# Delta-rule stage of a fused decoder: products of the next half ahead of the formings, two coupling buffers

## The chip, the cores and the metric

The kernel runs on one core of a Trainium2 chip. The metric is device time in microseconds for one launch, which is one program of fifteen stages over 16 batch rows of 128 tokens by 256 channels, all in float32 unless said. Only the first stage, `delta_stage` (L0_attn), is changed. In the profile PE is TensorE, PEld its weight load, DVE VectorE, ACT ScalarE and POOL GpSimd.

## What is computed

The first stage is a gated delta rule with 8 heads, 8 decay modes and key and value width 64:

```python
qr = _l2norm(_rotary(q, cos, sin)) * scale
kr = _l2norm(_rotary(k, cos, sin))
g = jnp.log(jnp.clip(tg * rho, 1e-06))
...
def step(S, inp):
    q_t, k_t, v_t, b_g, b_beta = inp
    S = S * jnp.exp(b_g)[..., None, None]
    kv = jnp.einsum('mbhk,mbhkv->mbhv', k_t, S)
    dv = (v_t[None] - kv) * b_beta[..., None]
    S = S + k_t[..., :, None] * dv[..., None, :]
    o_t = jnp.einsum('mbhk,mbhkv->mbhv', q_t, S)
    return (S, o_t)
...
o = jnp.einsum('tmbhv,hm->bthv', ys, mode_w)
return (o * gate).reshape(B, T, H * DV) @ Wo
```

The kernel does not scan over time. For each head and mode (a "chain") it forms a 128x128 matrix of decayed key-key products N and one of decayed key-query products, solves the unit triangular system with N in four blocks of 32 rows, and multiplies the solution by the query products.

## The kernel before

A turn of the stage is one batch row. A turn has two halves of 4 heads, so 32 chains each, in 8 groups of 4 chains (`GROUPS`). Halves are numbered `u`, and half `u` of a turn is first (`hf` 0) or second (`hf` 1). Every engine has its own program, and semaphores order them. A half passes through these steps:

- **Products** (`phase`): DVE rotates keys and queries (`rotate`, L1153 and L1158), POOL adds the two parts (`add_halves`, L698), PE makes decay exponents (L823, L824, L827) that ACT exponentiates (`decays`, L1019), PE makes the products (L844), and DVE multiplies both into the buffer `NB` (`take_products`, L1172). A pack is two groups. DVE issues `rotate(p+1, 0)`, group 2p, `rotate(p+1, 1)`, group 2p+1.
- **Lower blocks** (`take_lower`, ACT L1029): copies the 32x32 diagonal blocks, half after group 3 and half after group 7.
- **Inversion** (`invert`, DVE L1201 to L1210): a transpose, a copy, 60 linked small operations (L1207 and L1208 in turn) and a transpose back. In a first half, steps for the next batch row stand between the links.
- **Spread** (ACT L1039): puts the inverses into `Df`.
- **Forming** (`form`, PE L811, into PSUM banks 6 and 7): inverse times both matrices, one group at a time. ACT takes each group (`take_formed`, L1007 and three L1011): outputs to `NB`, couplings to the tensor `couplings`. One group must be taken before the next is formed.
- **Couplings, solutions** (`couple`, PE L736 and L863; ACT L1046): three block rows times four heads.
- **Outputs** (`output`, PE L878), `gated` (DVE L1218) and, once a turn, `project_out` (PE L886).

There is one N buffer, `NB[:, 0]`, so group i of half u+1 may be written only after group i of half u is formed (the wait on `formed` in `take_products`). PE therefore alternates: `form(u, i)`, `phase(u+1, i)`. The projections of the next batch row (`project_qk` L750, `project_bt` L756, `turn_qk` L775, `sum_logs` L765 to L767, `swap` L782, `project_v` L789, `project_gates` L797) stand among the couplings and outputs. POOL fills the right-hand sides (`fill`, L690) when the outputs of the half before are done. The order in each engine's program is written out by hand in its `turn`.

## Time and profile before

| | us |
|---|---|
| median of 3 runs | 6814.46 (6813.0 to 6816.96) |
| the profiled execution | 6818.27 |
| its span | 6816.5 |
| first stage, to its last `project_out` | about 2405 of the span |
| PE, DVE, ACT, POOL busy | 77%, 52%, 31%, 16% of the span |

The profiled execution is 3.8 us above the median. The first stage is about 35% of the span. Its steady part repeats once a batch row, and the page's shares mix it with fourteen other stages, so it is read from the timeline.

### The profile page before, as it was taken

What the parts mean: (1) busy time and instruction counts of PE and PEld (TensorE: products, weight loads), DVE (VectorE), ACT (ScalarE), POOL (GpSimd) and SP (SyncE); (2) the same over time, 40 slices, a digit from 0 to 9 for tenths busy, and PEclk for the clock granted to TensorE, in tenths of its full rate; (3) what the DMA queues carried; (4) which work ended last, traced back from release to release, by engine and by line L of the source; (5) the groups of instructions that cost most, each with busy time, mean ns of one, the idle gap of its engine ahead of it and who ended that gap; (6) DMA issues with size and microseconds to landing.
All of it is one profiled execution on the core that took longest, in us unless ns stands there. A gap on an engine that the chain in (4) does not pass through costs nothing. (4 is left out here: it accounts for less than half of the span.)

```text
span 6816.5 us, 79744 instructions
## 1 busy us (share of the span) xinstructions
PE 5226.9 (77%) x28029; PEld 3625.2 (53%) x28132; DVE 3569.8 (52%) x7608; ACT 2091.8 (31%) x3626; POOL 1070.7 (16%) x846
## 2 busy tenths in 40 slices
PE   2878878788787775999997877467577467788698
PEld 1666656666565544666665555234355245555454
DVE  6777777777777532000015545558734535444444
ACT  2544545454454411212212222211023322232111
POOL 1222222222222121000002222000011012221000
PEclk8988989889898886999998878655578578789799
DMA  0000000000000000000000000000000000000000
GB/s 32 1 1 1 1 2 1 1 1 2 1 1 1 1 23 36 13 25 12 25 0 7 0 29 6 11 3 1 10 25 1 4 8 0 21 6 1 12 18 24
DMA packets 13528, 63.44 MB, mean 9 GB/s; under 512 B 1168, under 2 KB 5648, under 8 KB 11152
## 3 DMA queue, kind: packets, MB, share of 16 engines
q1 hardware_dynamic: 13200, 59.17, 2.5%
q8 instruction: 193, 3.16, 0.2%
q14 instruction: 135, 1.11, 0.1%
HBM read 57.07 MB, written 2.10 MB: 9 GB/s over the span
## 5 line engine op out<-in xcount | busy, mean ns | idle before, releaser
L1467 PE MATMUL psum<-arena 128*128 128x512 f32 x1600 | 707.0, 596 | 58.4 <-DVE Y L1531 35.8
L811 PE MATMUL psum<-arena 128*128 128x256 f32 x2048 | 546.4, 413 | 140.7 <-ACT arena L1039 131.7
L1548 DVE SCALAR_TENSOR_TENSOR Y<-psum,arena,Y 128x256 f32<-128x256 f32 x416 | 172.5, 477 | 847.8 <-PE psum L1479 847.8
L1479 PE MATMUL psum<-arena 128*128 128x256 f32 x2624 | 583.0, 380 | 4.1 <-DVE arena L1572 4.1
L1479 PEld LDWEIGHTS psum<-arena 128*128 128x128 f32 x2624 | 499.1, 190 | 111.7 <-issue 43.5
L811 PEld LDWEIGHTS psum<-arena 128*128 128x128 f32 x2048 | 392.3, 202 | 288.9 <-issue 167.2
L144 POOL TENSOR_TENSOR arena<-arena,eps 128x4 f32<-128x4 f32 (+2 forms) x76 | 15.0, 197 | 3341.4 <-DVE arena L139 3341.4
L1467 PEld LDWEIGHTS psum<-arena 128*128 128x128 f32 x1600 | 304.5, 191 | 409.4 <-issue 341.7
L1172 DVE TENSOR_TENSOR arena<-psum,arena 128x1024 f32<-128x1024 f32 x256 | 313.3, 1224 | 392.0 <-PE psum L844 204.6
L698 POOL TENSOR_TENSOR arena<-arena 128x512 f32<-128x512 f32 x256 | 341.8, 1356 | 713.2 <-DVE arena L1158 713.2
L863 PE MATMUL psum<-arena 64*32 64x64 f32 (+2 forms) x6144 | 414.6, 220 | 0.0
L1513 ACT ACTIVATE arena<-psum,arena 128x512 f32<-128x512 f32 x256 | 175.9, 687 | 701.4 <-PE psum L1467 701.4
L422 PE MATMUL psum<-ident,arena 128*128 128x128 f32 x1280 | 216.9, 324 | 211.5 <-ACT arena L493 211.5
L402 PE MATMUL psum<-arena 128*128 128x512 f32 x640 | 358.9, 694 | 16.8 <-ACT arena L482 11.2
L863 PEld LDWEIGHTS psum<-arena 64*32 64x32 f32 (+2 forms) x6144 | 352.6, 109 | 20.7 <-issue 12.7
L1208 DVE TENSOR_TENSOR weights<-weights 128x30 f32<-128x30 f32 (+14 forms) x960 | 343.8, 358 | 32.6 <-DVE weights L1207 2.5
L1207 DVE TENSOR_TENSOR weights<-weights 128x30 f32<-128x30 f32 (+14 forms) x960 | 341.4, 356 | 34.9
L414 PEld LDWEIGHTS psum<-arena 128*128 128x128 f32 x2048 | 283.6, 216 | 102.3 <-issue 62.5
L844 PE MATMUL psum<-arena 64*128 64x256 f32 x2048 | 294.2, 406 | 28.1 <-POOL arena L698 28.1
L300 POOL TENSOR_TENSOR arena<-arena,weights 128x1024 f32<-128x1024 f32 x128 | 242.2, 1900 | 408.3 <-PE psum L402 343.1
L422 PEld LDWEIGHTS psum<-ident,arena 128*128 128x128 f32 x1280 | 178.1, 171 | 233.8 <-ACT arena L493 233.5
L414 PE MATMUL psum<-arena 128*128 128x17 f32 x2048 | 275.2, 278 | 33.4 <-ACT arena L490 33.4
(436 smaller groups left out, 8839.0 us busy)
## 6 DMA issues: line engine op xcount, KB each, us to landing
arena<-in_experts_L_ffn SPq DMA_DIRECT2D x8, 2052.0 KB, 8.5
arena<-in_ctxT SPq DMA_DIRECT2D x16, 512.0 KB, 3.3
arena<-in_experts_L_ffn SPq DMA_DIRECT2D x18, 384.0 KB, 3.1
weights<-in_w_L_attn SPq DMA_DIRECT2D x1, 3106.0 KB, 13.2
weights<-in_w_L_ffn SPq DMA_DIRECT2D x1, 3072.0 KB, 10.0
weights<-in_w_L_ffn SPq DMA_DIRECT2D x1, 2753.0 KB, 13.3
weights<-in_w_L_relu SPq DMA_DIRECT2D x1, 2436.0 KB, 8.9
X<-in_x SPq DMA_DIRECT2D x1, 2048.0 KB, 8.2
```

What stands on the lines that cost most here:

```text
L402: mm = nc.tensor.matmul(out[:, b * 4:b * 4 + 4, :], qT[:, c, u * P:(u + 1) * P], km[:, at % 2, b * 4:b * 4 + 4, :], start=True, stop=True)
L414: mm = nc.tensor.matmul(o_psum[:, c * HH + h, :], pT[:, j % 2, h, :], v, start=True, stop=True)
L422: mm = nc.tensor.transpose(pt_psum[:, h, :], pr[:, j % 2, h, :], k.ident[:, :])
L698: pool.tensor_tensor(both_, both_, t1[:, j, :, :], ALU.add).then_inc(s["rotated"], 1)
L811: mm = nc.tensor.matmul(ps[:, 6 + j // 2, (j % 2) * 2 * P:(j % 2 + 1) * 2 * P], Df[:, c, :], both(hf)[:, :, c, :], start=True, stop=True)
L844: mm = nc.tensor.matmul(ps[:, bank, m * 2 * P:(m + 1) * 2 * P], kq[rows, i // 2 % 2, at, 0, :], kq[rows, i // 2 % 2, at, :, :], start=True ...
L863: mm = nc.tensor.matmul(ps[n:n + Q, 4 + h, m * DK:(m + 1) * DK], couplings[0:n + Q, place(h, m), n - Q:n], ur[0:n + Q, h, m, :], start=Tru ...
L1172: dve.tensor_tensor(both(hf)[:, :, group, :].rearrange("p k c t -> p c k t"), products, bc(NB[:, 1 + hf, group, :], 2, 2), ALU.mult).then_ ...
L1207: linked(dve.tensor_tensor(part, bc(lanes[:, j + 1:, j], 2, j), bc(inv[:, j, 0:j], 1, below), ALU.mult))
L1208: linked(dve.tensor_tensor(inv[:, j + 1:, 0:j], inv[:, j + 1:, 0:j], part, ALU.add))
L1467: mm = nc.tensor.matmul(ps[:, bank, :], W[s][name][:, c, f * P:(f + 1) * P], xT[:, g, c, :], start=(c == 0), stop=(c == C - 1))
L1479: mm = nc.tensor.matmul(out, h[:, m % 2, f, u * P:(u + 1) * P], W[s]["w2"][:, f, :], start=(f == 0), stop=(f == FC - 1))
```

## The change

- `NB` has four planes in place of three, an N and an output plane for each half of a turn. `couplings` is gone: `take_formed` writes the couplings over N in the same plane, and a new `set_identities` (ACT, three copies of 32x1024) writes the identity blocks once a half. The wait of `take_products` on `formed` is gone.
- PE runs all 8 groups of `phase(u+1)` with only two formings of half u in them (behind groups 2 and 5). The other six formings follow the phase, with projections between them, and the couplings come behind these. ACT's order follows.
- `invert` works in place on `inv`, without the copy L1202. Its in-between steps stand at other links, and `first_part` and `second_part` move into it.
- POOL runs `add_halves` before `fill` in both halves.
- `xs` and `xT` move to the rest of the weights' region, and the stage's first memset and the three copies of L956 go.

In the diff `...` marks what is left out (renamed buffers in the same instructions).

```diff
-    xs, xT = A(D), A(C, P)
+    used = (k.words(stage) + 7) // 8 * 8
+    own = Arena(k.regions[k.stages.index(stage) % 2][:, used:], REGION - used)
+    xs, xT = own(D), own(C, P)
     v, gateT, bt, logs = A(W), A(PAIRS, P), A(2 * DHEADS * M), A(2 * DHEADS * M)
     qkT, qkS = A(2, PAIRS, P), A(2, PAIRS, P)
     kq, t1 = A(2, 4, 2, P), A(2, 4, P)
-    NB = A(1 + HALVES, CH, P)
-    couplings, Df = A(CH, P - Q), A(CH, P)
+    NB = A(2 * HALVES, CH, P)
+    Df = A(CH, P)
...
-        return NB[:, 0:hf + 2:hf + 1, :, :]
+        return NB[:, 2 * hf:2 * hf + 2, :, :]
...
+                add_halves(u + 1)
                 fill(u, g, 0)
-                add_halves(u + 1)
...
-                fill(u + 1, g, 1)
                 if more:
                     add_halves(u + 2)
+                fill(u + 1, g, 1)
...
-                    pe.wait_ge(s["outputs_formed"], u * GROUPS + i)
                     pe.wait_ge(s["couplings_formed"], u * GROUPS + i)
...
-                        pe.wait_ge(s["outputs_formed"], (u + 1) * GROUPS)
                         pe.wait_ge(s["couplings_formed"], (u + 1) * GROUPS)
+                        pe.wait_ge(s["identities_set"], u + 1)
...
-                                              couplings[0:n + Q, place(h, m), n - Q:n], ur[0:n + Q, h, m, :],
+                                              NB[0:n + Q, 2 * (u_odd), place(h, m), n:n + Q], ur[0:n + Q, h, m, :],
...
                 for i in range(GROUPS):
-                    form(u, 0, i)
                     phase(g, u + 1, 1, i)
+                    if i in (2, 5):
+                        form(u, 0, i // 3)
                 if more:
                     turn_x(g + 1)
-                couple(u, 1, (u + 1) * GROUPS + GROUPS - 1)
+                form(u, 0, 2)
+                form(u, 0, 3)
                 if more:
                     project_qk(g + 1)
-                couple(u, 2)
+                form(u, 0, 4)
                 if more:
                     project_bt(g + 1)
-                couple(u, 3)
+                for i in range(5, GROUPS):
+                    form(u, 0, i)
+                couple(u, 0, 1, (u + 1) * GROUPS + GROUPS - 1)
                 if more:
                     turn_qk(g + 1)
-                output(u, g, 0, 0)
+                couple(u, 0, 2)
                 if more:
                     sum_logs(g + 1)
+                    swap(g + 1)
+                couple(u, 0, 3)
+                output(u, g, 0, 0)
                 output(u, g, 0, 1)
-                if more:
-                    swap(g + 1)
                 for i in range(GROUPS):
-                    form(u + 1, 1, i)
                     if more:
                         phase(g + 1, u + 2, 0, i)
-                couple(u + 1, 1, (u + 2) * GROUPS + GROUPS - 1 if more else None)
-                if more:
-                    project_v(g + 1)
-                couple(u + 1, 2)
-                if more:
-                    project_gates(g + 1, (u + 3) * GROUPS)
-                couple(u + 1, 3)
+                    if i in (2, 5):
+                        form(u + 1, 1, i // 3)
+                for i in range(2, GROUPS):
+                    form(u + 1, 1, i)
+                    if more and i == 4:
+                        project_v(g + 1)
+                    if more and i == 6:
+                        project_gates(g + 1, (u + 3) * GROUPS)
+                couple(u + 1, 1, 1, (u + 2) * GROUPS + GROUPS - 1 if more else None)
+                couple(u + 1, 1, 2)
+                couple(u + 1, 1, 3)
                 output(u + 1, g, 1, 0)
                 output(u + 1, g, 1, 1)
...
-            for q in range(1, NQ):
-                rows = slice(q * Q, (q + 1) * Q)
-                nc.scalar.copy(couplings[rows, :, (q - 1) * Q:q * Q], bc(k.ident[rows, rows], 1, CH))
...
-                nc.scalar.copy(NB[:, 1 + hf, 4 * i:4 * i + 4, :], formed[:, :, 1, :]).then_inc(s["outputs_formed"], 1)
-                if i == 0:
-                    need(act, "solution_ready", u * (NQ - 1) * HALF)
+                nc.scalar.copy(NB[:, 2 * hf + 1, 4 * i:4 * i + 4, :], formed[:, :, 1, :])
...
-                    a = nc.scalar.copy(couplings[0:q * Q, 4 * i:4 * i + 4, (q - 1) * Q:q * Q],
+                    a = nc.scalar.copy(NB[0:q * Q, 2 * hf, 4 * i:4 * i + 4, q * Q:(q + 1) * Q],
                                        formed[0:q * Q, :, 0, q * Q:(q + 1) * Q])
...
-                if x == 0:
-                    need(act, "inverse_turned", n)
...
-                    a = nc.scalar.activation(lower[rows, 16 * x:16 * (x + 1), :], N_[rows, 16 * x:16 * (x + 1), rows],
+                    a = nc.scalar.activation(diagonal[rows, 16 * x:16 * (x + 1), :], NB[rows, 2 * hf, 16 * x:16 * (x + 1), rows],
...
+            def set_identities(n, hf):
+
+                act.wait_ge(s["lower_taken"], (n + 1) * 2)
+                for q in range(1, NQ):
+                    rows = slice(q * Q, (q + 1) * Q)
+                    a = nc.scalar.copy(NB[rows, 2 * hf, :, rows], bc(k.ident[rows, rows], 1, CH))
+                a.then_inc(s["identities_set"], 1)
...
-                    a = nc.scalar.copy(Df[rows, :, rows], Dc[rows, :, :])
+                    a = nc.scalar.copy(Df[rows, :, rows], diagonal[rows, :, :])
...
                 for i in range(GROUPS):
-                    take_formed(u, 0, i)
                     decays(u + 1, 1, i)
+                    if i in (2, 5):
+                        take_formed(u, 0, i // 3)
                     if i == 5:
-                        take_lower(u + 1, 0)
+                        take_lower(u + 1, 1, 0)
                 if more:
                     take_x(g + 1)
-                take_lower(u + 1, 1)
+                take_lower(u + 1, 1, 1)
+                take_formed(u, 0, 2)
+                take_formed(u, 0, 3)
+                if more:
+                    square(g + 1)
+                take_formed(u, 0, 4)
+                if more:
+                    sigmoids(g + 1)
+                for i in range(5, GROUPS):
+                    take_formed(u, 0, i)
+                if more:
+                    logarithms(g + 1)
+                set_identities(u + 1, 1)
                 solutions(u, 1)
                 if more:
-                    square(g + 1)
+                    take(g + 1, qkT, "qk_turned", "qkT_ready")
                 solutions(u, 2)
                 if more:
-                    sigmoids(g + 1)
-                solutions(u, 3)
-                if more:
-                    logarithms(g + 1)
-                    take(g + 1, qkT, "qk_turned", "qkT_ready")
                     round_sums(g + 1)
                     round_rest(g + 1)
                     take(g + 1, qkS, "swapped", "swapped_ready")
+                solutions(u, 3)
                 spread(u + 1)
                 for i in range(GROUPS):
-                    take_formed(u + 1, 1, i)
                     if more:
                         decays(u + 2, 0, i)
-                        if i == 5:
-                            take_lower(u + 2, 0)
+                    if i in (2, 5):
+                        take_formed(u + 1, 1, i // 3)
+                    if more and i == 5:
+                        take_lower(u + 2, 0, 0)
                 if more:
-                    take_lower(u + 2, 1)
+                    take_lower(u + 2, 0, 1)
+                for i in range(2, GROUPS):
+                    take_formed(u + 1, 1, i)
+                    if more and i == 4:
+                        take_v(g + 1)
+                if more:
+                    set_identities(u + 2, 0)
                 solutions(u + 1, 1)
-                if more:
-                    take_v(g + 1)
                 solutions(u + 1, 2)
                 solutions(u + 1, 3)
                 if more:
...
-                if not isinstance(n, int) or n:
-                    dve.wait_ge(s["formed"], (n - 1) * GROUPS + i + 1)
-                    if i == 0:
-                        need(dve, "lower_taken", n * 2)
...
-                need(dve, "inverse_ready", n)
-                linked(dve.transpose(lanes[:, :, :], lower.rearrange("p c t -> p t c")))
-                linked(dve.tensor_copy(inv[:, :, :], lanes[:, :, :]))
+                linked(dve.transpose(inv[:, :, :], diagonal.rearrange("p c t -> p t c")))
...
-                    linked(dve.tensor_tensor(part, bc(lanes[:, j + 1:, j], 2, j), bc(inv[:, j, 0:j], 1, below), ALU.mult))
+                    linked(dve.tensor_tensor(part, bc(inv[:, j + 1:, j], 2, j), bc(inv[:, j, 0:j], 1, below), ALU.mult))
...
-                dve.transpose(Dc.rearrange("p c j -> p j c"), inv[:, :, :].rearrange("p i j -> p j i")
+                dve.transpose(diagonal.rearrange("p c j -> p j c"), inv[:, :, :].rearrange("p i j -> p j i")
                               ).then_inc(s["inverse_turned"], 1)
 
             def gated(g, hf):
@@ -1301,18 +1316,16 @@
                     state["ch"].end()
                 steps = []
                 if more:
-                    steps += [(12, lambda: sum_squares(g + 1)), (34, lambda: scale_decays(g + 1)),
-                              (36, lambda: clip_decays(g + 1)), (40, lambda: normalise(g + 1)),
-                              (52, remember("views", lambda: split(g + 1))),
-                              (54, lambda: split_rest(g + 1, state["views"]))]
+                    steps += [(18, lambda: sum_squares(g + 1)), (20, lambda: scale_decays(g + 1)),
+                              (22, lambda: clip_decays(g + 1)), (32, lambda: normalise(g + 1)),
+                              (36, remember("views", lambda: split(g + 1))),
+                              (38, lambda: split_rest(g + 1, state["views"])),
+                              (50, lambda: first_part(g + 1)), (58, lambda: second_part(g + 1))]
                 if not first:
-                    steps += [(2, remember("ch", lambda: finish(g - 1))), (20, applied)]
+                    steps += [(2, remember("ch", lambda: finish(g - 1))), (14, applied)]
                 invert(u + 1, between(*sorted(steps, key=lambda x: x[0])))
-                if more:
-                    first_part(g + 1)
                 gated(g, 0)
                 if more:
-                    second_part(g + 1)
                     phase(g + 1, u + 2, 0)
                     invert(u + 2)
                 gated(g, 1)
```

PE, end of the first half's products, before: a forming and a group of products alternate, and the couplings (L736, L863) come directly behind `turn_x` (L742).

```order
L811 MATMUL psum<-arena 128x256 x4
L822 REGISTER_ALU
L823 MATMUL psum<-arena 128x512
L824 MATMUL psum<-arena,weights 128x512
L827 MATMUL psum<-weights,arena 128x128 x4
L844 MATMUL psum<-arena 128x256 x4
L739 REGISTER_ALU
L623 ISA
L742 MATMUL psum<-ident,arena 128x128 x2
L854 ISA
L736 MATMUL psum<-arena 128x1
L863 MATMUL psum<-arena 32x64 x8
```

The same place on PE in the changed kernel, where L841 is the products, L808 a forming, L748 `project_qk`:

```order
L841 MATMUL psum<-arena 128x256 x4
L737 REGISTER_ALU
L623 ISA
L740 MATMUL psum<-ident,weights 128x128 x2
L805 REGISTER_ALU
L808 MATMUL psum<-arena 128x256 x4
L805 REGISTER_ALU
L808 MATMUL psum<-arena 128x256 x4
L748 MATMUL psum<-weights 128x512 x4
L805 REGISTER_ALU
L808 MATMUL psum<-arena 128x256 x4
L754 MATMUL psum<-weights 128x128 x2
```

Three more formings stand behind these rows, and then the couplings.

PE, end of the second half's products in the changed kernel (L787 `project_v`, L795 `project_gates`, L734 and L860 a coupling; one row x12 is three formings):

```order
L841 MATMUL psum<-arena 128x256 x4
L808 MATMUL psum<-arena 128x256 x12
L784 REGISTER_ALU
L787 MATMUL psum<-weights 128x512 x2
L808 MATMUL psum<-arena 128x256 x8
L623 ISA
L795 MATMUL psum<-weights 128x128 x8
L808 MATMUL psum<-arena 128x256 x4
L734 MATMUL psum<-arena 128x1
L860 MATMUL psum<-arena 32x64 x8
```

Six formings now stand between the products and the couplings, where before one stood in front of each group.

ACT, end of a second half, before (L1029 `take_lower`, L1046 solutions, L1039 spread, L1000 gates):

```order
L1011 COPY arena<-psum 32x4x32
L1011 COPY arena<-psum 64x4x32
L1011 COPY arena<-psum 96x4x32
L1019 ACTIVATE arena<-psum 128x512
L1029 ACTIVATE weights<-arena 32x512 x4
L1046 ACTIVATE arena<-psum 32x512 x4
L995 COPY arena<-psum 128x512
L1046 ACTIVATE arena<-psum 32x512 x8
L1039 COPY arena<-weights 32x32x32 x4
```

ACT at the same place in the changed kernel (L1036 `set_identities`, L1052 solutions, L1045 spread):

```order
L1009 COPY arena<-psum 128x512
L1011 COPY arena<-psum 32x4x32
L1011 COPY arena<-psum 64x4x32
L1011 COPY arena<-psum 96x4x32
L1036 COPY arena<-ident 32x32x32 x3
L1052 ACTIVATE arena<-psum 32x512 x12
L1045 COPY arena<-weights 32x32x32 x4
L1002 ACT_TABLE_LOAD
L1002 ACTIVATE arena<-psum 128x512
```

The six takings stand between `take_lower` and the solutions, and the spread is behind them all.

## Rows read from the trace of the kernel before

**Rows 1.** DVE timeline: start us, length us, engine, line, operation, out<-in [idle before <-releaser]

```profile
1047.56 1.95 DVE L1201 STREAM_TRANSPOSE weights<-weights 128x1024 f32<-128x1024 f32 x1 [2.61 <-ACT weights L1029]
...
1091.93 1.23 DVE L1172 TENSOR_TENSOR arena<-psum,arena 128x1024 f32<-128x1024 f32 x1 [3.29 <-ACT arena L1019]
...
1116.54 1.22 DVE L1172 TENSOR_TENSOR arena<-psum,arena 128x1024 f32<-128x1024 f32 x1 [2.07 <-PE psum L844]
1120.38 1.97 DVE L1201 STREAM_TRANSPOSE weights<-weights 128x1024 f32<-128x1024 f32 x1 [2.61 <-ACT weights L1029]
...
1188.63 1.94 DVE L1201 STREAM_TRANSPOSE weights<-weights 128x1024 f32<-128x1024 f32 x1 [2.61 <-ACT weights L1029]
```

**Rows 2.** DVE timeline, end of a first, then a second half's inversion

```profile
1079.12 0.40 DVE L1218 SCALAR_TENSOR_TENSOR arena<-psum,arena 128x256 f32<-128x256 f32 x1
...
1122.38 0.69 DVE L1202 COPY weights<-weights 128x1024 f32<-128x1024 f32 x1
...
1137.33 0.40 DVE L1208 TENSOR_TENSOR weights<-weights 128x228 f32<-128x228 f32 x1
1137.76 1.11 DVE L1207 TENSOR_TENSOR weights<-weights 128x220 f32<-128x220 f32 x1
...
1149.98 0.38 DVE L1218 SCALAR_TENSOR_TENSOR arena<-psum,arena 128x256 f32<-128x256 f32 x1
1151.19 0.69 DVE L1153 TENSOR_TENSOR arena<-arena,weights 128x512 f32<-128x512 f32 x1 [0.83 <-issue]
```

**Rows 3.** PE timeline, the wait behind that inversion

```profile
1150.42 3.78 PE L886 MATMUL psum<-weights,arena 128*128 128x256 f32 x8 [13.16 <-DVE arena L1218]
```

**Rows 4.** timeline of all engines, the last half of the last turn

```profile
2366.60 1.97 PE L811 MATMUL psum<-arena 128*128 128x256 f32 x8 [1.23 <-ACT arena L1011]
2368.60 0.58 ACT L1007 COPY arena<-psum 128x512 f32<-128x512 f32 x1 [2.15 <-PE psum L811]
2369.08 0.57 ACT L1011 COPY arena<-psum 32x128 f32<-32x128 f32 x3
...
2369.80 1.97 PE L811 MATMUL psum<-arena 128*128 128x256 f32 x8 [1.24 <-ACT arena L1011]
...
2385.80 0.16 PE L736 MATMUL psum<-arena 128*128 128x1 bf16 x1 [1.24 <-ACT arena L1011]
...
2399.21 3.71 PE L878 MATMUL psum<-arena 128*64 128x128 f32 x64
...
2402.97 0.42 DVE L1218 SCALAR_TENSOR_TENSOR arena<-psum,arena 128x256 f32<-128x256 f32 x1 [50.39 <-PE psum L878]
```

**Rows 5.** timeline of all engines, one pack of products

```profile
1162.26 2.94 POOL L698 TENSOR_TENSOR arena<-arena 128x512 f32<-128x512 f32 x2 [5.62 <-DVE arena L1158]
...
1165.26 1.13 PE L844 MATMUL psum<-arena 64*128 64x256 f32 x8 [0.85 <-POOL arena L698]
...
1166.53 1.23 DVE L1172 TENSOR_TENSOR arena<-psum,arena 128x1024 f32<-128x1024 f32 x1 [0.78 <-PE psum L844]
...
1168.27 0.68 DVE L1158 TENSOR_TENSOR arena<-arena,Y 128x512 f32<-128x512 f32 x1
```

**Rows 6.** ACT timeline, the identity blocks at the stage's start

```profile
70.34 3.15 ACT L956 COPY arena<-ident 32x1024 f32<-32x1024 f32 x3
```

**Rows 7.** ACT timeline, the last `take_lower` before a second half's inversion

```profile
1117.80 2.55 ACT L1029 ACTIVATE weights<-arena 32x512 f32<-32x512 f32 x4 [1.44 <-DVE arena L1172]
```

**Rows 8.** groups of PE by line, 1047.5-1137.3 us (xcount | busy us, mean ns | idle)

```profile
L750 PE MATMUL psum<-weights,arena 128*128 128x512 f32 x8 | 3.7, 605 | 0.0
...
L797 PE MATMUL psum<-arena,weights 128*128 128x128 f32 x16 | 2.1, 281 | 0.0
L782 PE MATMUL psum<-arena,weights 128*128 128x512 f32 x4 | 2.0, 618 | 0.0
```

**Rows 9.** PE timeline, first forming behind a first half's inversion

```profile
1085.07 3.77 PE L811 MATMUL psum<-arena 128*128 128x256 f32 x8 [4.86 <-ACT arena L1039]
```

**Rows 10.** stretch: PE, PEld, DVE, ACT, POOL busy us (x), granted clock, DMA share, GB/s

```profile
1083.00:1085.50 2.50, 0.43 (x1) 0.43 (x2) 2.50 (x4) 1.92 (x2) 0.67 (x2) 0.50 0.00 0
```

27 lines of the change are left out of this document (12 added, 15 removed).

## The prediction

> **What bounds the kernel now.** I read the timeline of DVE first, since the stage repeats once a batch row. A second half's inversion starts 72.8 us behind a first half's, and the next first half's 68.25 us behind that [rows 1]. A turn is 141.1 us. Inside the second half, group 0 of the products is taken at 1091.93, group 7 at 1116.54, and the inversion starts 3.84 behind group 7: so 28.45 us from the first taking to the inversion [rows 1]. The inversion ends with L1218 at 1149.98, 29.6 us behind its start [rows 2], and PE waits 13.16 us for it [rows 3]. So one loop sets the time: products alternating with formings, `take_lower`, inversion, spread. The couplings and outputs of PE lie in the inversion's shade with 13 us to spare. The change takes the formings out of the products and puts six of eight into that shade. The question is whether the shade holds them.
>
> **What a forming costs alone.** The last half of the last turn shows it, since no products stand beside it there. Formings start 3.20 us apart, 1.97 on PE and the rest ACT's L1007 and L1011, because banks 6 and 7 must be emptied before the next [rows 4]. The first coupling starts 3.20 behind the last forming (2382.60, to 2385.80), the twelve head steps of couplings take 13.4 (2385.80 to 2399.21), and the outputs 3.76 to the start of L1218 [rows 4].
>
> **The new chain of PE and ACT in a second half**, counted from the inversion's start, which is the end of `take_lower` on ACT. ACT takes group 2, which PE formed while ACT was busy: 1.05, and PE starts group 3 at 1.2. Five formings at 3.20 are 16.0. `project_v` (the shape of L782, 2.0) and `project_gates` (2.1) [rows 8] stand between formings and mostly fill waits for ACT; past 1.2 us of wait each they cost 0.5, so 1.0. Couplings can start at 18.2. `set_identities` is three copies like L956, 3.15 us [rows 6], and holds the first solution back, but PE is busy 4.5 us with the first block row, so it costs nothing; with less cover it would cost 3.15. Couplings 13.4, outputs 3.76: o is ready at 35.4.
>
> The inversion itself becomes shorter: L1202 goes (0.77 from its start to the next link [rows 2]), and `fill` no longer runs under it. Under L690 four links take about 1.1 us where the link in front took 0.40 [rows 2], which is 2.9 us. It would end at 29.6 - 0.8 - 2.9 = 25.9. The chain ends 9.5 us later. DVE has `gated` in its queue in front of `rotate`, so the whole products phase of the next half stands behind the outputs. Those 3.7 us of DVE are worth nothing.
>
> The Trainium skill speaks of the same thing in "SBUF — State Buffer", section "SBUF: two separate sides": VectorE with two SBUF inputs and GpSimd take one port pair in turn, for the whole instruction. By the rows four links ran slower and none was held for good; either way a `fill` taken out of the inversion returns a few us there, all of it inside the 9.5 us of slack.
>
> From o ready: L1218 and the loop's end 1.2 (1149.98 to 1151.19 [rows 2]), two rotations of two instructions at 0.6, 2.4, and from the last rotation's end to the taking 4.35 (POOL starts 0.1 behind it at 1162.26 and takes 2.94, PE 1.13, the taking is at 1166.53 [rows 5]). Group 0 is taken at 35.4 + 8.0 = 43.4.
>
> **Products without formings.** They are not bound by PE now but by a loop through four engines. From the end of `rotate(p,1)` to the taking of the next pack's group it is 4.35, then the taking 1.14 and the next rotation 1.28: the next end is at 1168.95, so 6.75 a pack [rows 5], where before a pack took 2/7 of 24.6, 7.0 [rows 1]. Groups 0, 2 and 4 are taken at 0, 6.75 and 13.5. At group 5 ACT must wait for a forming, take it (1.05) and do a `take_lower` (2.55 [rows 7]) before the decay of group 6: forming ends 3.6 behind the taking of group 4, the copies at 4.7, `take_lower` at 7.2, decay at 7.8. Group 6 is taken at 7.9, group 7 (exponents 0.8, products 1.1) at 9.9. So group 7 at 23.4 and the inversion at 23.4 + 3.84 = 27.2, against 28.45. Freeing the products from the formings is worth 1.2 us a half.
>
> Second half: 43.4 + 27.2 = 70.6, before 68.25: **+2.3**.
>
> **First half.** Here `project_qk` (3.7) delays group 4 by 2.2 net; `project_bt` and the sigmoid are hidden by ACT's takings. Couplings can start at 1.2 + 16.0 + 2.2 = 19.4. Between them stand `turn_qk` (eight 128-column matmuls, half of L797's sixteen: 1.0), `sum_logs` (twelve: 1.5) and `swap` (L782, 1.85) [rows 8]. With 13.4 and 3.76 o is ready at 40.9. The inversion with its steps lasted 31.6 (1047.56 to L1218 at 1079.12 [rows 1, 2]); less 0.8 and with `first_part` and `second_part` inside it is some 32.6, and it must also wait for ACT's rounding of `sum_logs`, at about 31.5, which makes it 38. Still under 40.9. L1218 and start of the rotation 0.4, then 6.75: group 0 at 48.1, and with 27.2 it is 75.3, before 72.8: **+2.5**.
>
> **The clock.** All this is at the full 2.4 GHz. Before, PE ran without a gap in the products; the granted clock fell behind its waits for DVE: after 4.86 idle a forming took 3.77 instead of 1.97 [rows 4, 9], at a granted clock of 0.50 [rows 10]. The changed kernel has no 13 us wait, but in a first half PE waits about 5 us from its last output to the first product, in a second half about 3.5, in front of each pack about 3, and at `take_lower` 3. The first surely drops the clock, the others perhaps. A drop doubles L844 in the loop (1.1) or a forming in the chain (1.8). Bounds: nothing, where those costs lie in other waits, and 8 us a turn, if each of some six waits does it at 1.3. I take two drops a turn that cost: **+2.4**, nearer to the lower bound because in the last half formings kept the full clock across gaps of 1.24 us [rows 4].
>
> **The sum.** 2.3 + 2.5 + 2.4 = 7.2 us a turn, 15 times from the first inversion of turn 0 to the last: +108. At the ends: L956 goes from the start (3.15 [rows 6]), the first half has no chain in front of it (about -4), and the last half starts its formings at a better clock (two of them took double: -3.6). About -10. 6818.3 + 98 = 6916 in the profiled execution, 3.8 less in the median: **6912 us**.
>
> **The rivals.**
> 1. As forecast, the PE and ACT chain takes the place of the inversion as the bound, with some drops of the clock. 6912. Chance 0.50.
> 2. The same without further cost of the clock: 4.8 x 15 - 10 = +62: 6876. For it: no gap in the formings is above 2 us. Chance 0.20.
> 3. The clock falls in every pack. PE is busy 3.7 us and idle 3.05 in each, and a first half's wait of 4.86 was enough [rows 9]. Then 4.8 + 8 = 12.8 a turn, +182: 6996. The Trainium skill, "TensorE: Matmul & The Clock Gate", section "HAM oscillation", tells of a kernel that was throttled anew behind every wait between its bursts. Chance 0.15.
> 4. Faster: the chain fits under the inversion, and DVE stays the bound. Then the second half is 25.9 + 8.0 + 27.2 = 61.1 and the first 32.6 + 7.15 + 27.2 = 67.0, which is 13 a turn less: about 6610. It decides at a chain shorter by 9.5 us in the second half and 8.3 in the first; half of the way there, 2.4 us a half, is break-even. It needs formings at some 2 us apart, where [rows 4] have 3.20. A partial gain counts here. Chance 0.11.
> 5. No change: the longer chain and the shorter products cancel. Chance 0.04.
>
> **How the numbers follow.** The forecast is the likeliest case. The range takes cases 1 and 2 with 1 us a turn of doubt, and most of 3: 6860 to 6990. A measurement of this kernel can tell about 0.2% (14 us) from no change. Faster 0.11, same 0.04, slower 0.85.
>
> **What the changed profile would show.** L1201 starts about 75 and 71 us behind each other. L1218 waits for PE's L875, not at once behind the transpose, by some 9 us in a second half and 3 in a first. Formings L808 behind the products start 3.2 apart with gaps "<-ACT L1011". L1189 is spaced 6.8 a pack. L1223 and L1225 have no 1.1 us links. PE waits less than 6 us anywhere, and the granted clock says which of 1 to 3 it is. I am wrong if PE still waits for the inversion in a second half, if formings are closer than 3.2, or if DVE takes the products of a half in under 20 us.

## The result and the profile after

| | us |
|---|---|
| before, median of 3 | 6814.46 |
| after, median of 3 | 6987.04 (6981.84 to 7007.31) |
| ratio | 1.026, 95% interval 1.0228 to 1.0292 |
| profiled execution, its span | 7007.31, 7005.5 |
| forecast | 6912, range 6860 to 6990 |

The change makes the kernel slower, as forecast, but by 173 us where 98 were forecast. By the ratio to the kernel before the time is 1.026 x 6814 = 6991, which is just outside the range. The profiled execution was the slowest of the three.

I call the stretch that begins at an inversion with steps between its links a "first half" and the other one a "second half", as the prediction does. DVE's timeline of the changed kernel over one second half (columns as in [rows 1]):

```profile
1039.84 1.94 DVE L1217 STREAM_TRANSPOSE weights<-weights 128x1024 f32<-128x1024 f32 x1 [2.61 <-ACT weights L1027]
...
1063.79 2.07 DVE L1225 STREAM_TRANSPOSE weights<-weights 128x1024 f32<-128x1024 f32 x1
1080.38 0.42 DVE L1233 SCALAR_TENSOR_TENSOR arena<-psum,arena 128x256 f32<-128x256 f32 x1 [14.52 <-PE psum L875]
1083.37 0.69 DVE L1174 TENSOR_TENSOR arena<-arena,weights 128x512 f32<-128x512 f32 x1 [2.56 <-issue]
...
1091.07 1.22 DVE L1189 TENSOR_TENSOR arena<-psum,arena 128x1024 f32<-128x1024 f32 x1 [1.71 <-PE psum L841]
...
1111.62 1.22 DVE L1189 TENSOR_TENSOR arena<-psum,arena 128x1024 f32<-128x1024 f32 x1 [4.53 <-ACT arena L1019]
1115.08 1.22 DVE L1189 TENSOR_TENSOR arena<-psum,arena 128x1024 f32<-128x1024 f32 x1 [2.24 <-PE psum L841]
1118.91 1.93 DVE L1217 STREAM_TRANSPOSE weights<-weights 128x1024 f32<-128x1024 f32 x1 [2.61 <-ACT weights L1027]
```

The inversion is over at 1065.9, 26.0 after its start (forecast 25.9), and then DVE waits 14.52 us for PE's outputs. Where PE used to wait for the inversion [rows 3], DVE now waits for the outputs. From one inversion to the next it is 79.07 us, where it was 68.25 [rows 1]. A first half takes 74.4 (it was 72.8). The first stage ends at 2598 us of the span where it ended at 2405; the other fourteen stages take 4407 us where they took 4411.

PE's timeline inside the same second half shows what the prediction lacked:

```profile
1040.94 1.99 PE L808 MATMUL psum<-arena 128*128 128x256 f32 x8 [3.06 <-ACT arena L1011]
1044.08 1.99 PE L808 MATMUL psum<-arena 128*128 128x256 f32 x8 [1.14 <-ACT arena L1011]
...
1054.27 1.89 PE L808 MATMUL psum<-arena 128*128 128x256 f32 x8
1057.45 1.08 PE L860 MATMUL psum<-arena 64*32 64x64 f32 x16
...
1059.68 1.40 PE L860 MATMUL psum<-arena 64*32 64x64 f32 x16
1061.13 1.91 PE L860 MATMUL psum<-arena 64*32 64x64 f32 x16
...
1072.90 1.56 PE L860 MATMUL psum<-arena 128*32 128x64 f32 x16
...
1076.62 3.71 PE L875 MATMUL psum<-arena 128*64 128x128 f32 x64
```

The couplings begin at 1057.35, 17.5 behind the inversion's start (forecast 18.2). They are twelve head steps (one block row of one head each, a row of 16 matmuls L860 here), and they have no gap. Yet the third head step slows down (1.40), and from 1061.13 to 1072.9 each takes 1.91 instead of 1.08. The twelve take 19.3 us, not 13.4. The table by stretch, cut at the couplings (columns as in [rows 10]), has the clock beside it:

```profile
1039.84:1057.35 17.51, 12.94 (x60) 9.92 (x61) 16.06 (x43) 6.97 (x26) 0.00 (x0) 1.00 0.00 0
1057.35:1076.62 19.27, 19.27 (x204) 17.44 (x204) 7.83 (x21) 9.31 (x14) 0.00 (x0) 0.65 0.01 2
```

The granted clock was full while the formings ran with PE busy 12.94 of 17.51 us, and 0.65 on average in the couplings, in which PE was busy without a pause: it went from the full level (2.4 GHz) to half of it and back. The couplings of every second half fall in this way. Those of the first halves, where the longer `project_qk` stands between the formings, keep 1.08 in fourteen of the fifteen turns in which a next batch row follows; the second head step of the first half behind this one:

```profile
1138.97 1.08 PE L860 MATMUL psum<-arena 64*32 64x64 f32 x16
```

The groups of PE, after and then before, give the sum over the whole stage:

```profile
L841 PE MATMUL psum<-arena 64*128 64x256 f32 x2048 | 354.0, 473 | 246.4 <-POOL arena L696 246.4
L860 PE MATMUL psum<-arena 64*32 64x64 f32 (+2 forms) x6144 | 520.1, 250 | 0.0
```

```profile
L863 PE MATMUL psum<-arena 64*32 64x64 f32 (+2 forms) x6144 | 414.6, 220 | 0.0
L844 PE MATMUL psum<-arena 64*128 64x256 f32 x2048 | 294.2, 406 | 28.1 <-POOL arena L698 28.1
```

The same 6144 coupling matmuls take 105.5 us more, the products 59.8 more.

The rhythm of the formings alone does not decide it. In the kernel before, the last half of [rows 4] has nearly the same rhythm, six formings 3.20 apart with gaps of 1.24 at the full clock and PE less busy (11.79 of 19.20 us), and the couplings behind them kept the full clock:

```profile
2366.60:2385.80 19.20, 11.79 (x49) 8.62 (x49) 0.00 (x0) 6.32 (x24) 0.00 (x0) 1.00 0.00 1
2385.80:2399.21 13.41, 13.41 (x204) 12.13 (x205) 0.00 (x0) 6.48 (x11) 0.00 (x0) 1.00 0.01 1
```

In the changed kernel's own last half, behind eight formings 3.14 apart, they fell again (20.8 us). What sets these two apart no run tells.

### The profile page after: what moved, and what is told of

It reads as the page before. It is cut to its first block and busy times, and to the rows that moved or that the text cites. A ratio compares the mean times of both kernels' runs of the same rounds, so it can differ in the third digit from the quotient of the medians.

```text
span 7005.5 us, 79394 instructions
## 1 busy us (share of the span) xinstructions
PE 5363.7 (77%) x28132; PEld 3704.0 (53%) x28132; DVE 3454.2 (49%) x7576; ACT 2207.6 (32%) x3719; POOL 1034.3 (15%) x845
## 5 line engine op out<-in xcount | busy, mean ns | idle before, releaser
L808 PE MATMUL psum<-arena 128*128 128x256 f32 x2048 | 526.8, 402 | 176.8 <-ACT arena L1011 175.6
L1492 PE MATMUL psum<-arena 128*128 128x256 f32 x2624 | 583.0, 380 | 4.1 <-DVE arena L1585 4.1
L808 PEld LDWEIGHTS psum<-arena 128*128 128x128 f32 x2048 | 385.5, 197 | 307.5 <-ACT arena L1011 223.4
L841 PE MATMUL psum<-arena 64*128 64x256 f32 x2048 | 354.0, 473 | 246.4 <-POOL arena L696 246.4
L860 PE MATMUL psum<-arena 64*32 64x64 f32 (+2 forms) x6144 | 520.1, 250 | 0.0
L860 PEld LDWEIGHTS psum<-arena 64*32 64x32 f32 (+2 forms) x6144 | 448.0, 129 | 12.3 <-issue 6.6
L841 PEld LDWEIGHTS psum<-arena 64*128 64x128 f32 x2048 | 213.1, 225 | 306.9 <-POOL arena L696 144.6
L1223 DVE TENSOR_TENSOR weights<-weights 128x30 f32<-128x30 f32 (+14 forms) x960 | 318.7, 332 | 33.0
L1222 DVE TENSOR_TENSOR weights<-weights 128x30 f32<-128x30 f32 (+14 forms) x960 | 318.0, 331 | 30.9
L1009 ACT COPY arena<-psum 128x512 f32<-128x512 f32 x256 | 150.1, 586 | 497.9 <-PE psum L808 497.2
```

What stands on the lines that cost most here:

```text
L808: mm = nc.tensor.matmul(ps[:, 6 + j // 2, (j % 2) * 2 * P:(j % 2 + 1) * 2 * P], Df[:, c, :], both(hf)[:, :, c, :], start=True, stop=True)
L841: mm = nc.tensor.matmul(ps[:, bank, m * 2 * P:(m + 1) * 2 * P], kq[rows, i // 2 % 2, at, 0, :], kq[rows, i // 2 % 2, at, :, :], start=True ...
L860: mm = nc.tensor.matmul(ps[n:n + Q, 4 + h, m * DK:(m + 1) * DK], NB[0:n + Q, 2 * (u_odd), place(h, m), n:n + Q], ur[0:n + Q, h, m, :], sta ...
L1222: linked(dve.tensor_tensor(part, bc(inv[:, j + 1:, j], 2, j), bc(inv[:, j, 0:j], 1, below), ALU.mult))
L1223: linked(dve.tensor_tensor(inv[:, j + 1:, 0:j], inv[:, j + 1:, 0:j], part, ALU.add))
L1492: mm = nc.tensor.matmul(out, h[:, m % 2, f, u * P:(u + 1) * P], W[s]["w2"][:, f, :], start=(f == 0), stop=(f == FC - 1))
```

## The experiments

Each was timed beside the kernel before, which stood at 6813 to 6818. The halves are the most common intervals between inversions in the profiled execution.

| kernel | median us | ratio (95%) | second / first half |
|---|---|---|---|
| before | 6814 | | 68.3 or 69.2 in turn / 72.9 |
| after | 6987 | 1.0228 to 1.0292 | 79.1 (83.2 in 3 of 16) / 74.4 |
| warm | 6967 | 1.0208 to 1.0242 | 74.9 (83.2 in 2 of 16) / 75.3 |
| rotate_first | 6957 | 1.0191 to 1.0225 | 74.7 / 79.0 (71.5 in 4 of 15) |
| warm_rotate | 6850 | 1.0038 to 1.0091 | 71.3 (77.6 to 79.2 in 4 of 16) / 72.2 |
| phase_warm | 7068 | 1.0357 to 1.0415 | 81.0 / 75.9 |
| four_in | 6825 | 1.0003 to 1.0032 | 71.4 to 73.7 / 68.7 to 70.5 |
| five_in | 6870 | 1.0060 to 1.0094 | 67.9 / 78.8 |
| five_normalise | 6827 | 1.0006 to 1.0034 | 68.0 / 71.4, or 75.2 to 75.9 in 7 of 15 |
| six_in | 6856 | 1.0038 to 1.0071 | 64.4 to 68.1 / 79.5 |
| six_rotate | 6905 | 1.0113 to 1.0147 | 69.1 / 78.8 or 79.9 in turn |
| pool_order | 6771 | 0.9912 to 0.9945 | 65.5 / 73.1 |
| alternate | **6727** | 0.9856 to 0.9889 | 64.7 / 71.8 |
| rotate_early | 6782 | 0.9932 to 0.9965 | 68.3 / 71.6 |

**warm: keep PE busy between the formings.** Four matmuls of 128x512 bf16 into a free bank in front of formings 4 to 7:

```diff
+ for _ in range(4 if i >= 4 else 0):
+     nc.tensor.matmul(ps[:, 5, :], ident_h, later_h[:, :, :], start=True, stop=True)
  pe.wait_ge(s["couplings_formed"], u * GROUPS + i)
```

> The changed kernel with one addition: in front of the wait of each of the formings 4 to 7 of a half PE makes four 128x512 bfloat16 products of constants into bank 5, whose result nothing reads (0.22 us each at the full clock, in a gap of 1.14 us). Clock theory: the granted clock falls to 0.50 in a second half's couplings because PE works only some 60% of the time while it forms; with the gaps filled the couplings take 13.4 us again instead of 19.2, a turn is 6 us shorter, and the time is about 6900 us. Rival, the fall comes from the long waits for POOL and take_lower or from the position in time, not from the formings' gaps: the couplings stay at 19 us and the time within 15 us of 6987.

PE's timeline of a second half:

```profile
1025.54 1.99 PE L810 MATMUL psum<-arena 128*128 128x256 f32 x8 [3.06 <-ACT arena L1013]
...
1036.12 1.99 PE L810 MATMUL psum<-arena 128*128 128x256 f32 x8 [0.28 <-ACT arena L1013]
...
1043.77 1.08 PE L862 MATMUL psum<-arena 64*32 64x64 f32 x16
...
1056.08 1.08 PE L862 MATMUL psum<-arena 128*32 128x64 f32 x16
```

The gap in front of a forming shrinks from 1.14 to 0.28 us, the couplings run at 1.08 throughout, and the half gets 4.2 us shorter: 5.9 less in the couplings, 1.7 more in front of them, for the dummy matmuls also lengthen the formings. The wait of 3.06 behind `take_lower` stands as it did, so that wait doesn't slow the couplings by itself. It is so in 13 of the 15 second halves in front of the last turn's; in two the couplings still fell. The time came out at 6967, above the 6900 hoped for, because of those 1.7 us, because first halves got 0.9 longer and because of the two that fell.

**rotate_first: the gating behind the next rotations.** `gated` is issued after the first four rotation instructions of the following phase:

```diff
-                gated(g, 0)
-                if more:
-                    phase(g + 1, u + 2, 0)
+                    phase(g + 1, u + 2, 0, lambda: gated(g, 0))
```

> The changed kernel with one instruction of DVE moved: gated stands behind the first four rotation instructions of the next products phase instead of in front of them. Queue theory: from the outputs to group 0 it is 10.7 us in a second half (loop end 2.6, rotations 2.4, POOL, PE) and 8.0 in a first; with the rotations and POOL's additions done while PE still couples it is about 5 in either, bounded by ACT's spread and table loads. 8 to 9 us a turn less: about 6855 us. Rival, ACT's spread and decays arrive no earlier than group 0 does now: within 30 us of 6987.

DVE's timeline:

```profile
1034.97 2.02 DVE L1227 STREAM_TRANSPOSE weights<-weights 128x1024 f32<-128x1024 f32 x1
1037.94 0.69 DVE L1174 TENSOR_TENSOR arena<-arena,weights 128x512 f32<-128x512 f32 x1 [0.94 <-issue]
...
1051.55 0.42 DVE L1235 SCALAR_TENSOR_TENSOR arena<-psum,arena 128x256 f32<-128x256 f32 x1 [11.11 <-PE psum L875]
1051.89 0.68 DVE L1174 TENSOR_TENSOR arena<-arena,weights 128x512 f32<-128x512 f32 x1
```

DVE now reaches the end of its loop without having waited, and it costs 0.94 us instead of 2.56. The second half is 4.4 us shorter. But in most first halves the couplings now fall to the half clock, and those halves are 7.5 us longer. That was not expected, and it ate the gain. The order of PE in first halves is the changed kernel's, where the couplings held. The time, 6957, is where the rival had it (within 30 us of 6987), but for this reason and not for the rival's.

**warm_rotate: both edits above in one kernel.**

> Both single repairs of the changed kernel together: the dummy matmuls of warm in the gaps of the formings (second halves 79.1 to 74.9, first 74.4 to 75.2) and the gating behind the first rotations of rotate_first (second 79.1 to 74.7, but first halves 79 in eleven of fifteen). Theory, the two named costs (the clock that falls near the couplings, and the end of DVE's loop behind a blocked wait) are all that parts the changed kernel from the sum without a clock term: second halves 71 to 72.5, first halves 72 to 73.5, 144.5 a turn against 153.5, 6987 less 135: 6835 to 6880, about where the prediction stood for a clock that holds (6876). Rival, the half clock only moves to another place in the loop: first halves 76 to 79 here too, 6910 to 6950.

6850, as the theory said and not as the rival did. Two costs part the changed kernel from the prediction's own case 2 (a clock that holds, 6876): the slow couplings and the loop's end (with the gating moved, the first product of a second half's phase is back at 1.13 as well). Neither repair alone brought more than 30 us, both together 137. rotate_first alone left the couplings of the second halves slow and slowed those of most first halves; with the dummies in it too, no first half falls, and four second halves still do.

**phase_warm: the same dummies, elsewhere.** Ten in front of each pack's first product, where PE waits for POOL; the waits on `products_taken` and `solution_ready` move in front of them:

```diff
+ for _ in range(10 if i % 2 == 0 else 0):
+     nc.tensor.matmul(ps[:, 5, :], ident_h, later_h[:, :, :], start=True, stop=True)
  pe.wait_ge(s["rotated"], (n * NPACKS + i // 2 + 1) * 2)
```

> The changed kernel with ten matmuls of 128x512 bf16 into a free PSUM bank in front of each pack's first product, where PE otherwise waits about 3 us for POOL (some 2.1 us of work at the full clock; the formings and their 1.2 us gaps stay as they are). It tells from which idle time the clock falls. Theory A, the formings' gaps just before: couplings still at 1.9 us a head step, only the products at 2.08 get their 1.1 back: second half 78 to 79, time 6965 to 6990. Theory B, the waits in the products some 20 us earlier count as much: couplings back at 1.08, 19.3 us becomes 13.4, second half 72 to 73, time about 6895. If the extra work is not hidden, a pack grows by up to 2 us and the time goes above 7050.

PE's timeline, couplings of a second half:

```profile
1077.19 1.08 PE L867 MATMUL psum<-arena 64*32 64x64 f32 x16
...
1079.42 1.91 PE L867 MATMUL psum<-arena 64*32 64x64 f32 x16
...
1089.22 1.91 PE L867 MATMUL psum<-arena 96*32 96x64 f32 x16
```

The couplings are as slow as before, in every second half. So of the idle time that was filled, the one between the formings just in front of them counts, and that in the products does not. The extra work was not hidden, hence 7068: theory A for the clock, but with the surcharge that was named. The 3 us of wait that the expectation counted on stand in front of the first pack alone (mostly 3.1 to 3.8 or 5.19 in the changed kernel, and 0.9 to 1.6 in front of the second); the third and fourth have this:

```profile
1102.35 1.13 PE L841 MATMUL psum<-arena 64*128 64x256 f32 x8 [0.70 <-POOL arena L696]
```

**four_in, five_in: more formings among the products.** Behind groups 1 to 4, then behind groups 0 to 4.

```diff
-                    if i in (2, 5):
-                        form(u, 0, i // 3)
+                    if i in (0, 1, 2, 3, 4):
+                        form(u, 0, i)
```

> The changed kernel with four formings inside the products (behind groups 1, 2, 3 and 4) instead of two (behind 2 and 5), and four behind them instead of six. Chain theory: two formings of 3.2 us less in the chain of each half, and no forming in front of the lower blocks at group 5 (1.0 us), so some 7 us a half and 14 a turn less: about 6775 us. Rival, the products get longer by what the chain loses, since PE is their bound: within 30 us of 6987.

> The changed kernel with five formings among the products (behind groups 0 to 4) and three behind them. The chain of PE and ACT is then 9.6 us shorter than in the changed kernel: 25.8 us in a second half and 31.3 in a first, if the couplings have the full clock, which is no longer than the inversion (25.9 and 32.6). Theory 'the chain is the bound and the clock falls in the couplings' (it fell in four_in too): the chain is about 6 us too long in many halves, so 3.2 us a half come off four_in's intervals at most where the chain binds: about 68 us in a second half, 67 to 70 in a first, 6740 to 6780 in all. If the clock stays up: 61 and 67 us, near 6640. Rival 'formings cost as much among the products as behind them': no gain on four_in, 6825 or above.

A shorter chain gives most of the time back at first (four_in: 6825, ratio 1.0003 to 1.0032), but not the 6775 expected: the couplings of its second halves still go to 1.91, all of them. With five the second half falls again, to 67.9, and the couplings there keep 1.08 in 13 of 15. But the first half is 78.8. PE's timeline of five_in:

```profile
1225.16 1.08 PE L860 MATMUL psum<-arena 64*32 64x64 f32 x16
1230.10 1.97 PE L773 MATMUL psum<-ident,arena 128*128 128x128 f32 x8 [3.87 <-DVE arena L1242]
1232.00 1.91 PE L860 MATMUL psum<-arena 96*32 96x64 f32 x16
```

PE comes to `turn_qk` 3.87 us before DVE's `normalise`, which stands at link 32, and everything from there to 1243 runs at the half clock. Both of my theories missed this wait. The time, 6870, is where the rival had it (6825 or above), but second halves did gain, which the rival denied.

**five_normalise: that step earlier.**

```diff
-(32, lambda: normalise(g + 1))
+(26, lambda: normalise(g + 1))
```

> five_in with one step of DVE moved: `normalise` stands at link 26 of the inversion and not at 32. In five_in PE came to `turn_qk` 3.87 us before it and then ran 16 us at the half clock; the interval behind the inversion with steps was 78.8 us where four_in mostly had 69 to 70. Theory, this wait and the clock that falls behind it are five_in's loss: the wait shrinks below 1 us, the couplings keep 1.08, the interval falls to 67.5 to 70, and the time to 6870 less about 15 x 10: 6710 to 6740. Rival, the clock falls in that chain anyway, from the gaps of the formings: only the 3.9 us come back, interval 75, 6815.

The wait fell to 1.23 us. Yet the first half is 71.4 or 75.8, not 67.5 to 70, and the time 6827, nearer to the rival's 6815 than to 6710 to 6740. In a half of 71.4 the chain is 34.3 us from the inversion's start to o ready where 31.3 were worked out: the wait, and the first forming (2.92) and `project_qk` (4.41) at a lower clock behind the wait for `take_lower`. The halves of 75.8 have the same wait of 1.23, and PE's timeline shows what makes them longer. First a half of 71.4, then one of 75.8:

```profile
1053.67 1.09 PE L773 MATMUL psum<-ident,arena 128*128 128x128 f32 x8 [1.23 <-DVE arena L1242]
1054.99 1.08 PE L860 MATMUL psum<-arena 96*32 96x64 f32 x16
...
1340.13 1.97 PE L773 MATMUL psum<-ident,arena 128*128 128x128 f32 x8 [1.23 <-DVE arena L1242]
1342.04 1.91 PE L860 MATMUL psum<-arena 96*32 96x64 f32 x16
```

In the first the following couplings keep 1.08, as the theory said; in the second the clock falls there in spite of the short wait, as the rival said, and the second block row runs at 1.91. Why it falls in some halves and not in others stays open.

**six_in, six_rotate.** Six formings inside and the steps earlier; six_rotate has the edit of rotate_early (below) too.

```diff
-if i in (0, 1, 2, 3, 4):
+if i in (0, 1, 2, 3, 4, 5):
...
-(18, lambda: sum_squares(g + 1)), (20, lambda: scale_decays(g + 1)),
-(22, lambda: clip_decays(g + 1)), (32, lambda: normalise(g + 1)),
+(12, lambda: sum_squares(g + 1)), (22, lambda: scale_decays(g + 1)),
+(24, lambda: clip_decays(g + 1)), (20, lambda: normalise(g + 1)),
```

> Six formings among the products (behind groups 0 to 5), two behind them, the sum of squares at link 12 and `normalise` at link 20. The chain of PE and ACT is 3.2 us shorter again, so that it ends before the inversion even with a slow clock in part of it. Theory, DVE's inversion is then the bound, and products in front of the first forming still get group 0 at 8.0 us (12.07 in the alternate order, where group 0 waits behind the spread and forming 0): 25.9 + 8.0 + 29.3 (seven groups 3.64 apart and 3.84) = 63.2 in a second half, 32.6 + 7.2 + 29.3 = 69 in a first: 132.2 a turn, 6680 to 6710, below the alternate order's 6727. Rival: PE waits for `normalise` again, or the first forming at the half clock delays the groups: 6750 to 6800.

> six_in with the first pack's rotations for the next half moved into the inversion without steps, as in rotate_early. There they brought nothing (group 0 waited for spread and forming 0, 11.76 us behind the last transpose's start, 12.07 without) and made the inversion 4 us longer (two rotations 2.4, one link 1.25 instead of 0.24 beside POOL, and the waits). Here group 0's product stands in front of the forming, so theory says that group 0 is taken some 3 us behind the inversion's end instead of 8: 4 us lost, 5 to 6 won: 10 to 30 us less than six_in. Rival: PE's `project_out` and the exponents behind it at the half clock hold group 0 back, nothing is won and 4 us are lost in 15 halves: 60 us more than six_in.

six_in comes out at 6856, above the 6680 to 6710 of its theory and the 6750 to 6800 of its rival. Second halves are 1.2 to 5 us above the 63.2 expected, first halves 10 us above their 69. ACT's and PE's timeline of six_in, a first half:

```profile
1072.20 0.31 ACT L975 ACTIVATE arena<-arena 128x128 f32<-128x128 f32 x1 [6.26 <-DVE arena L1254]
1072.54 3.15 ACT L1033 COPY arena<-ident 32x1024 f32<-32x1024 f32 x3
1075.71 2.04 ACT L1049 ACTIVATE arena<-psum 32x512 f32<-32x512 f32 x4
```

```profile
1070.43 1.97 PE L773 MATMUL psum<-ident,arena 128*128 128x128 f32 x8 [1.08 <-DVE arena L1240]
1076.47 1.91 PE L860 MATMUL psum<-arena 96*32 96x64 f32 x16
```

ACT has the logarithms in its queue in front of `set_identities` and the first solutions, and they wait 6.26 us for DVE's `clip_decays`, which my edit had put at link 24, two links later than it was. The second block row starts 4 us late, at a clock that had fallen already. The step that is late is the next one of the same side chain (projection, sum, root, normalise, clip, logarithm), whose steps stand at fixed links. Twice PE's chain was cut, and each time another of them was late. six_rotate made second halves 3 us longer and won nothing: nearer to its rival (60 us more than six_in) than to its theory, at 49 more.

**alternate: the old order of PE and ACT with the new buffers.** Formings alternate with the products and the projections stand between the couplings again; N in two planes, the inversion in place and POOL's order stay.

```diff
                for i in range(GROUPS):
+                   form(u, 0, i)
                    phase(g, u + 1, 1, i)
-                   if i in (2, 5):
-                       form(u, 0, i // 3)
```

> All buffers, the inversion in place, its steps and POOL's order as in the changed kernel, but PE and ACT in the order of the kernel before: forming i, then products i, and the couplings directly behind, with the projections among them. Order theory (six formings in a row behind the products are what costs): the inversion bounds again, and what it saves is now visible: 0.8 us in each half, 2.9 us of fill in a second half and some of the first and second part in a first, 5 to 7 us a turn less than before, so about 6720 us. Rival, the buffers or the identity blocks cost: it stays above 6814 us.

6727, faster than both kernels, and as expected. PE waits for the inversion again, and DVE no longer for the outputs:

```profile
1103.78 0.38 DVE L1213 SCALAR_TENSOR_TENSOR arena<-psum,arena 128x256 f32<-128x256 f32 x1
1103.93 4.21 ACT L1037 COPY arena<-weights 32x1024 f32<-32x1024 f32 x4 [8.95 <-DVE weights L1205]
1104.21 3.06 PEld L883 LDWEIGHTS psum<-weights,arena 128*128 128x128 f32 x8 [9.63 <-DVE arena L1213]
```

The second half is 3.6 us shorter than before: the 3.7 us that the prediction found in the inversion and called worth nothing behind the longer chain. Under the old order they are worth all of it.

**pool_order: the kernel before with POOL's order alone** (in both halves).

```diff
-                fill(u, g, 0)
                 add_halves(u + 1)
+                fill(u, g, 0)
```

> The kernel before with one part of the change alone: POOL adds the halves of the next products in front of the fill. Theory: most of what the alternate order gained (6727 against 6816) is this: no fill under a second half's inversion gives back 2.9 us there, and none beside the first rotations of the next half about 1 us in a first half: 3.9 a turn, 58 us, about 6757. The copy that is left in place (0.8 us in each inversion, 24 us in all) explains the rest. Rival: the gain of the alternate order is from the second buffer and the projections' and steps' new places: then 6800 or above here.

Second halves fall by 2.8 us, as expected from the four links that took 1.11 [rows 2] beside these four fills of the kernel before:

```profile
1137.35 4.71 POOL L690 TENSOR_TENSOR arena<-arena 128x512 f32<-128x512 f32 x4 [26.79 <-PE psum L878]
```

First halves gain nothing (73.1), so the time is 6771 and not 6757. Swapping these two calls in both halves of the kernel before gives half of what alternate does.

**rotate_early: alternate with the next phase's first rotations inside the inversion without steps.**

```diff
-for j in range(2):
+for j in range(0 if hf else 2):
     rotate(g, n, hf, 0, j)
...
-invert(u + 2)
+invert(u + 2, between((48, lambda: rotate(g + 1, u + 3, 1, 0, 0)),
+                      (54, lambda: rotate(g + 1, u + 3, 1, 0, 1))))
```

> The alternate order (6727) with the first pack's four rotations for a second half's products moved into the inversion in front of them, between links 48 and 54. Theory: with PE's chain shorter than the inversion, DVE's loop is the bound, and of the 8 us from the inversion's end to the taking of group 0 the rotations only move (2.4) but the wait for POOL and PE behind them (4.35 us) becomes hidden: 4.3 us in 16 halves, 70 us: about 6660. The intervals from a first half's inversion to a second half's fall from 71.7 to 67.4, the others stay at 64.7. Rival: POOL's adding beside the inversion slows its links by as much (as the fill did, 2.9 us): 6705 or more.

(The text on record names the wrong interval: the rotations lie in the inversion that begins a second half, so 64.7 was to fall.) It rose to 68.3, and the time is 6782, as the rival had it (6705 or more). The timeline of POOL and DVE at the end of that inversion, and DVE at group 0:

```profile
1127.99 2.48 POOL L696 TENSOR_TENSOR arena<-arena 128x512 f32<-128x512 f32 x2 [30.56 <-DVE arena L1159]
1128.10 1.25 DVE L1203 TENSOR_TENSOR weights<-weights 128x84 f32<-128x84 f32 x1
1129.39 1.16 DVE L1202 TENSOR_TENSOR weights<-weights 128x58 f32<-128x58 f32 x1
1130.59 0.22 DVE L1203 TENSOR_TENSOR weights<-weights 128x58 f32<-128x58 f32 x1
...
1143.05 1.22 DVE L1169 TENSOR_TENSOR arena<-psum,arena 128x1024 f32<-128x1024 f32 x1 [7.33 <-ACT arena L1011]
```

Group 0 waits 7.33 us for ACT: in this order it stands behind the spread (4.21) and forming 0, so the rotations were never what it waited for. The inversion got 4 us longer, 2.4 by the rotations and 1.9 by the two links beside POOL. I had the wrong releaser for group 0 there.

## Why the prediction was right or wrong

- **What becomes the bound: right.** DVE waits for the outputs (14.52), PE not for the inversion. Formings start 3.14 apart behind each other (forecast 3.20), couplings at 17.5 (18.2), the inversion lasts 26.0 (25.9), a product phase, from group 0 to the inversion, 26.3 in a first half and 27.8 in a second (27.2 for both). A first half takes 74.4, and the sum said 75.3: o is ready at 40.1 and not 40.9, the first product at the half clock takes that back (group 0 at 48.1, as forecast), and the phase is 0.9 shorter.
- **The step that failed: "Couplings 13.4".** I took their length from the last half of the last turn [rows 4], where the clock holds, and let the clock fall only in the work directly behind waits of PE, as in [rows 9, 10]. It fell in the middle of the gap-free couplings, behind formings 3.1 to 3.6 apart. They took 19.3: +5.9 in a second half. My clock term had 2.4 a turn, for other places. The row that I used as comfort, formings that keep the clock across 1.24 us gaps, was true of the formings and said nothing sure of the work behind them. In the second halves the gaps of that pattern have a part in the fall a few us later: warm takes the fall away in 13 of 15 by filling them, phase_warm in none by filling others. But they are not all of it, for in [rows 4] itself the couplings behind the same pattern held. What else it takes stays open.
- **The loop's end: 1.2 forecast** for the gating and the turn of the loop, from a DVE that had not waited [rows 2]. Behind a wait of 14.5 us the turn itself is 2.56 instead of 0.83, and from the gating to the rotation it is 2.99, +1.8; rotate_first shows 0.94 where the wait is moved behind it.
- **Products at the half clock**: the first product of a phase takes 2.08 instead of 1.13, +1.0 before group 0 is taken; in a second half the second and the last are about as slow, and the phase is 27.8, +0.6. These had a place in the clock term. Waits of 3 us and more, which I had in front of each pack, stand in front of the first pack alone.
- **The sum again.** 5.9 + 1.8 + 1.0 + 0.6 less 0.7 for the couplings' earlier start is 8.6 in a second half; measured are 79.1 against 70.6, 8.5. With -0.9 in the first half, 0.8 a turn for three halves of 83 us, and less the 2.4 of the clock term it is 6.0 a turn. Fifteen turns are 90 us; the profiled execution is 91 above its forecast of 6916. That the two agree so well is partly luck. The turn before is 141.7 on average and not 141.1, since its second halves are 68.3 and 69.2 in turn and [rows 1] show one of 68.25, which takes 8 us off; and the ends of the stage brought -2 and not -10, among them the last turn's couplings, which fell too. In the three halves of 83 us the first two formings behind `take_lower` took 3.78 each: there the clock fell earlier as well.
- **Rival 3**, the clock that falls in every pack, came closest in time (6996) and was wrong in mechanism: in a second half the middle five of a phase's eight products run at 1.13, and behind the first pack PE waits 0.7 to 1.6 us for POOL, not 3.05. The Trainium skill, "TensorE: Matmul & The Clock Gate", section "A second HAM failure mode: psum-queue depth-cycling", also tells of a second kind, in which PE pauses briefly between groups of matmuls over and over. The formings with their 1.14 us gaps are nearer to that than to the long wait that I cited the page for; that the slow stretch comes in gap-free work behind the groups is what this trace shows (1.91 from 1061.13 on).
- **The other skill page.** I wrote that no link was "held for good" by POOL's fill. The rows agree better with a lock than I allowed: four fills took 4.71 us and exactly four links 1.11; two adds took 2.48 and two links 1.25 and 1.16 (rotate_early). One link per POOL instruction, each about as long as that instruction. The Trainium skill, "SBUF — State Buffer", section "SBUF: two separate sides", says that the pair is held for the whole instruction, and the trace agrees.
- **Rival 4** needed a chain shorter by 9.5 us. The kernels with four to six formings inside shortened it, but a side chain of projections or the clock took its place each time; none has a median under 6825.

## What to carry to other kernels

Before moving work into the shade of another engine, work out the chain there with the clock at either level, and don't take a duration for safe because one place in the trace has it: here 3.1 us steps with 1.1 us gaps cost nothing themselves, and the gap-free work behind them was 5.9 us slower in every second half, though the one such place in the kernel before had held the clock. Ask of every part of a change whether it pays alone: the new buffers, the in-place inversion and POOL's order gained 87 us, and the new order of PE and ACT that they made possible lost 260. When a long chain is cut, look for fixed places (a step tied to a link, a step ahead in a queue) that were early enough only because the chain was long.

## What was unexpected of the hardware

- The granted clock falls while PE is fully busy. The first two head steps of the couplings take 1.08, the third 1.40, the next six 1.91, then one 1.56 and two 1.08. Filling the gaps in front of them took the fall away (warm), so the slow work need not be the work beside the gaps.
- A half clock that is taken away at one place can come up at another: rotate_first left the second halves shorter and put 7.5 us into eleven first halves. A kernel can have two lengths for the same stretch (71.4 and 75.8 in five_normalise, with the same wait of 1.23 us), and one half tells little.
- The turn of DVE's loop costs 0.83 to 0.94 us when DVE was busy up to it and 2.56 when its last instruction had waited long (2.73 in five_in). PE's next instruction behind its own loop's end waits 1.71 there (2.01 in rotate_first). Why, no run tells.
